# Last mixture: rows fetched by indirect DMA through a slot table, two dense tiles in front, weights split in the attention

## The reference

```
logits = x2 @ router_w;  probs = softmax(logits);  top_p, top_e = top_k(probs, 2)
for every chosen (token, expert e):
    h = gelu(x2[token] @ w_in[e] + b_in[e])
    y = (h @ w_out[e] + b_out[e]) * p          # p: the probability of that choice
    out[token] += y
x = x + out
```

## Time and profile before

| | |
|---|---|
| timed runs | 896.3, 900.05, 902.11 us |
| profiled execution | span 906.0 us; no time of its own is given beside the span |
| TensorE | 836.0 us busy, 92% of the span, mean granted clock 0.958 |
| VectorE (DVE) | 670.9 us, 74% |
| ScalarE (ACT) | 485.3 us, 54% |
| GpSimd (POOL) | 251.8 us, 28% |
| DMA | 115.93 MB, mean 128 GB/s |

### The profile page before, as it was taken

How to read it: one execution, slowest core, us unless ns; L and a number is a source line. 1 busy time by engine, 2 the same in 40 slices (tenths; PEclk the granted TensorE clock), 3 DMA queues, 4 the chain that set the end, 5 groups by cost and what they waited for, 6 DMA issues and landing times. The chain is left out here.

```text
span 906.0 us, 17871 instructions
## 1 busy us (share of the span) xinstructions
PE 836.0 (92%) x6115; PEld 773.1 (85%) x6115; DVE 670.9 (74%) x1359; ACT 485.3 (54%) x1022; POOL 251.8 (28%) x211
## 2 busy tenths in 40 slices
PE   7988999998797999999999999979799878999977
PEld 5877899998587999999999999965788745989867
DVE  3883799998676447888888888968687777775657
ACT  2653333333373557677777777753455542645643
POOL 7420233223003550034433333330122201432530
PEclk8988999999898999999999999998899987999999
DMA  8990000000402228577777777725000040534325
GB/s 303 294 291 3 1 1 0 1 1 1 150 2 100 100 84 299 225 231 232 232 232 232 226 222 228 255 25 185 1 1 1 1 175 31 162 100 130 106 86 171
DMA packets 60067, 115.93 MB, mean 128 GB/s; under 512 B 8482, under 2 KB 45956, under 8 KB 53220
## 3 DMA queue, kind: packets, MB, share of 16 engines
q1 hardware_dynamic: 48420, 97.48, 32.4%
q0 software_dynamic: 9408, 15.53, 7.0%
q10 hardware_dynamic: 2176, 2.10, 0.7%
HBM read 84.29 MB, written 30.79 MB: 127 GB/s over the span
## 5 line engine op out<-in xcount | busy, mean ns | idle before, releaser
L143 PE MATMUL e_ps_h<-e_xh,e_w1h 128*128 128x256 f32 (+1 forms) x496 | 141.7, 286 | 5.5 <-issue 5.5
L144 PE MATMUL e_ps_h<-e_xl,e_w1h 128*128 128x256 f32 (+1 forms) x496 | 139.2, 281 | 0.0
L145 PE MATMUL e_ps_h<-e_xh,e_w1l 128*128 128x256 f32 (+1 forms) x496 | 138.9, 280 | 0.0
L1996 POOL DMA_INDIRECT accumulated<-m_yo,m_token x39 | 77.7, 1992 | 194.1 <-ACT m_yo L2136 166.4
L143 PE MATMUL e_ps_o<-e_w2h,e_hh 128*128 128x256 f32 x440 | 122.3, 278 | 0.0
L2116 ACT ACTIVATE e_hf<-e_ps_h,e_b1s 128x256 f32<-128x256 f32 (+1 forms) x248 | 97.9, 446 | 45.1 <-PE e_ps_h L145 42.2
L145 PE MATMUL e_ps_o<-e_w2h,e_hl 128*128 128x256 f32 x440 | 121.8, 277 | 0.0
L144 PE MATMUL e_ps_o<-e_w2l,e_hh 128*128 128x256 f32 x440 | 121.8, 277 | 0.0
L894 POOL TENSOR_TENSOR at_pr<-at_pr,at_inv 128x1168 f32<-128x1168 f32 (+2 forms) x48 | 58.7, 1238 | 225.9 <-DVE at_inv L826 225.9
L143 PEld LDWEIGHTS e_ps_h<-e_xh,e_w1h 128*128 128x128 f32 x496 | 94.9, 191 | 5.7 <-issue 5.7
L144 PEld LDWEIGHTS e_ps_h<-e_xl,e_w1h 128*128 128x128 f32 x496 | 94.9, 191 | 0.0
(11 more groups left out here) (427 smaller groups left out, 2338.3 us busy)
## 6 DMA issues: line engine op xcount, KB each, us to landing
e_w1s<-in_m_w SPq DMA_DIRECT2D x24, 1024.0 KB
e_w2s<-in_m_w SPq DMA_DIRECT2D x24, 1024.0 KB, 7.2
slots_in<-zero SPq DMA_DIRECT2D x20, 258.0 KB, 9.4
e_xin<-slots_in SPq DMA_DIRECT2D x16, 258.0 KB
last_slots_in<-zero SPq DMA_DIRECT2D x14, 258.0 KB, 7.7
d_xin<-last_slots_in SPq DMA_DIRECT2D x10, 258.0 KB
d_results<-last_results SPq DMA_DIRECT2D x10, 256.0 KB, 4.5
as_wk<-in_a_wk SPq DMA_DIRECT2D x2, 1024.0 KB, 9.2
```

Source lines behind the costliest of these rows:

```text
L143: nc.tensor.matmul(out, lh, rh, start=start, stop=False)
L144: nc.tensor.matmul(out, lh, rl, start=False, stop=False)
L145: return nc.tensor.matmul(out, ll, rh, start=False, stop=stop)
L1996: nc.gpsimd.indirect_dma_start(out=g.acc[a], out_offset=bass.IndirectOffsetOnAxis(ap=token[:, n, a:a + 1], axis=0), in_=yo[:, q, a, :], in ...
```

## The change

- **Dense tiles.** 2 tiles in front instead of 4 (`FRONT = 2`), 2 at the back as before. So 12 tiles are routed instead of 10: 12 pairs and 7 singles.
- **Weights.** A new class `Matrices` loads and splits all 16 weight matrices of the last mixture during the second attention: in each of 16 tiles ACT casts one matrix (128x512) after the exponential, and POOL subtracts after the normalisation. The loads and splits in `prepare` and in the dense front go.
- **Slot table.** Nothing is scattered before the routed tiles and no slots are zeroed. SP stores the normalised rows of tiles 0 to 11 to HBM in order (3 DMAs of 512 KB), with one row of zeros ahead. DVE makes one-hot tables of each choice's unit and lane; POOL multiplies the unit table with the row number; 24 matmuls (`find`) accumulate the row number of every slot. DVE turns that into two integer tables, `source` and `target`.
- **Fetch.** POOL fetches each block of 128 rows with an indirect DMA through `source`, 4 tiles ahead (`AHEAD = 4`), and stores results through `target`, in one program.
- **Front.** One semaphore step per expert; the low part of the hidden values is made on POOL; ACT scales the second product into its own buffer for each expert, and DVE adds the eight buffers to X during the routed tiles. The counts' product comes in turn 3 instead of turn 0, and `find` in turn 8, ahead of the last second product.
- **Results.** ACT no longer scales the routed results; DVE multiplies by the probability as it adds them at the end, in 6 parts of two tiles, four operations a part. The bias product for the dense tiles moves from the front to turn 3 of the back.

```diff
-        rows = self.g.xs1.rearrange("(a p) d -> p a d", p=P)
-        for a in range(0, rows.shape[1], 2):
-            sp.dma_start(rows[:, a:a + 2, :], self.g.zero[:]).then_inc(self.g.s_zeroed1, 16)
...
+            if matrices and (not static or 0 <= t < NT):
+                matrices.scalar(act, t, q)
...
+            if matrices:
+                matrices.gpsimd(pool, t, q)
...
+class Matrices:
+
+    COUNT = 2 * E
+
+    def __init__(self, nc, ctx, L, w, sem):
+        self.nc, self.w = nc, w
+        self.W = DK * L.hid
+        sb = lambda name, shape, dt=FP: ctx.enter_context(nc.sbuf_tensor("d_" + name, shape, dt))
+        self.high, self.low = sb("w_high", [P, self.COUNT, self.W], FR), sb("w_low", [P, self.COUNT, self.W], FR)
+        self.raw = sb("w_raw", [P, 2, self.W])
+        self.s_raw = [sem(f"d_w_loaded{q}") for q in range(2)]
+        self.s_high, self.s_low = sem("d_w_high"), sem("d_w_low")
+
+    def sync(self, sp):
+        for i in range(self.COUNT):
+            wait(sp, self.s_low, i - 1)
+            sp.dma_start(self.raw[:, i % 2, :], self.w["w2" if i % 2 else "w1"][i // 2]).then_inc(self.s_raw[i % 2], 16)
+
+    def scalar(self, act, i, q):
+        wait(act, self.s_raw[q], 8 * i + (8 if q else 16))
+        self.nc.scalar.copy(one(self.high, i), self.raw[:, q:q + 1, :]).then_inc(self.s_high, 1)
+
+    def gpsimd(self, pool, i, q):
+        wait(pool, self.s_high, i + 1)
+        self.nc.gpsimd.tensor_tensor(one(self.low, i), self.raw[:, q:q + 1, :], one(self.high, i), ALU.subtract).then_inc(self.s_low, 1)
+
+
     CT = 4
+    FRONT = 2
     REST = 2
-    DT = CT + REST
+    DT = FRONT + REST
     RT = NT - DT
...
+    SECOND = RT * P
+    EMPTY = TOPK * SECOND
+    UC = 32
+    AHEAD = 4
...
+                    sp.dma_start(g.xs1[0:1, :], g.zero[0:1, 0, 0:D]).then_inc(self.s_rows, 16)
+                    rows = g.xs1[1:1 + self.RT * P].rearrange("(t p) d -> p t d", p=P)
+                    for c in range(self.RT // CT):
+                        ts = slice(c * CT, (c + 1) * CT)
+                        sp.wait_ge(s_xn, CT * (c + 1))
+                        sp.dma_start(rows[:, ts, :], xn[:, ts, 0:D]).then_inc(self.s_rows, 16)
...
-        for i, is_it in enumerate((self.is1, self.is2)):
-            link(dve, v.tensor_tensor(tmp, slot, rows(is_it), ALU.mult))
-            link(dve, v.tensor_reduce(self.inv[:, 0:RT], tmp, AX.X, ALU.add))
-            v.tensor_copy(self.at[:, i, :], self.inv[:, 0:RT, 0]).then_inc(self.s_k, 1)
+
+        both = slot.rearrange("p (a t) e -> p a (t e)", a=1).to_broadcast([P, TOPK, RT * E])
+        link(dve, v.tensor_tensor(self.masked[:].rearrange("p c t e -> p c (t e)"), both,
+                                  self.chosen[:, :, 0:RT, :].rearrange("p c t e -> p c (t e)"), ALU.mult))
+        link(dve, v.tensor_reduce(self.at[:], self.masked[:].rearrange("p c t e -> p (c t) e"), AX.X, ALU.add))
+        link(dve, v.tensor_copy(self.at_i[:], self.at[:]))
+        link(dve, v.tensor_scalar(self.lane[:], self.at_i[:], P - 1, None, ALU.bitwise_and))
+        link(dve, v.tensor_tensor(self.unit[:], self.at[:], self.lane[:], ALU.subtract))
+        v.tensor_tensor(self.is_unit[:], self.unit[:].to_broadcast([P, TOPK * RT, self.UC]),
+                        self.unit_no[:].to_broadcast([P, TOPK * RT, self.UC]), ALU.is_equal).then_inc(self.s_is, 1)
+        for i in range(TOPK):
+            ns = slice(i * RT, (i + 1) * RT)
+            v.tensor_tensor(self.lanes[:, ns, :], self.lane[:, ns, :].to_broadcast([P, RT, P]),
+                            self.lane_no[:].to_broadcast([P, RT, P]), ALU.is_equal).then_inc(self.s_lanes, 1)
...
+        dve.wait_ge(self.s_found, 1)
+        v.tensor_copy(self.row[:], ps_i)
+        link(dve, v.tensor_scalar(self.back[:], ps_i, self.SECOND + 0.5, -float(self.SECOND), ALU.is_gt, ALU.mult))
+        link(dve, v.tensor_tensor(self.back[:], self.row[:], self.back[:], ALU.add))
+        v.tensor_copy(self.source[:], self.back[:]).then_inc(self.s_source, 1)
+        link(dve, v.scalar_tensor_tensor(out=self.none[:], in0=self.row[:], scalar=0.5, in1=self.empty_no[:], op0=ALU.is_lt, op1=ALU.mult))
+        link(dve, v.scalar_tensor_tensor(out=self.none[:], in0=self.row[:], scalar=-1.0, in1=self.none[:], op0=ALU.add, op1=ALU.add))
+        v.tensor_copy(self.target[:], self.none[:]).then_inc(self.s_target, 1)
...
+                    def find(i):
+                        if i == 0:
+                            pe.wait_ge(s_units, 1)
+                        pe.wait_ge(self.s_lanes, i + 1)
+                        for n in range(i * RT, (i + 1) * RT):
+                            last = nc.tensor.matmul(ps_i, self.lanes[:, n, :], unit_rows[:, n, :], start=n == 0, stop=n == TOPK * RT - 1)
+                        if i == TOPK - 1:
+                            last.then_inc(self.s_found, 1)
...
+                        if r == 1:
+                            pe.wait_ge(r_b1, TILES)
+                            nc.tensor.transpose(ps_w, wt[:, RT:NT, :].rearrange("p t e -> p (t e)"), g.ident[:]).then_inc(s_wtt, 1)
+                        if r == 3:
+                            pe.wait_ge(s_wtt_sb, 1)
+                            pe.wait_ge(self.s_b, 16 * 3)
+                            for a in range(0, DT, 2):
+                                last = nc.tensor.matmul(ps_b[:, a // 2], wtt[:], b2d[0:DT * E, a:a + 2, :], start=True, stop=True)
+                            last.then_inc(s_bias, 1)
...
+                    def weighted(r):
+                        if r == 0:
+                            act.wait_ge(s_wt, 1)
+                        act.wait_ge(s_m2, r + 1)
+                        for a in range(FRONT):
+                            last = a_.activation(fy[:, r, a, :], ps_o[:, r % 4, a, :], ACT.Copy, scale=wt[:, FULL + a, r:r + 1])
+                        last.then_inc(s_ev, 1)
...
                     def add_results(i):
                         each = RT // PARTS
-                        ts = slice(i * each, (i + 1) * each)
-                        x = g.X[:, ts, :]
                         dve.wait_ge(s_y[i], 32)
-                        v.tensor_tensor(x, x, y[:, 0, ts, :], ALU.add).then_inc(s_sum, 1)
-                        dve.wait_ge(s_sum, i + 1)
-                        v.tensor_tensor(x, x, y[:, 1, ts, :], ALU.add).then_inc(s_fin, 1)
+                        for c, (p, added) in enumerate(((self.p1, s_sum), (self.p2, s_fin))):
+                            if c:
+                                dve.wait_ge(s_sum, i + 1)
+                            for t in range(i * each, (i + 1) * each):
+                                x = g.X[:, t, :]
+                                last = v.scalar_tensor_tensor(out=x, in0=y[:, c, t, :], scalar=p[:, t], in1=x, op0=ALU.mult, op1=ALU.add)
+                            last.then_inc(added, 1)
+                        if r == E - PARTS:
+                            dve.wait_ge(s_bias, 1)
+                            dve.wait_ge(s_x, E)
+                            x = g.X[:, FULL:NT, :]
+                            v.tensor_tensor(x, x, ps_b[:, 1], ALU.add).then_inc(s_bias_x, 1)
+                        if r == E - PARTS + 1:
+                            dve.wait_ge(b_x, REST * r)
+                            x = g.X[:, RT:FULL, :]
+                            v.tensor_tensor(x, x, ps_b[:, 0], ALU.add).then_inc(s_bias_x, 1)
+                            dve.wait_ge(s_bias_x, 2)
...
+                    gp = nc.gpsimd
+
+                    def low_hidden(r):
+                        pool.wait_ge(s_hh, r + 1)
+                        wait(pool, s_m2, r - 1)
+                        gp.tensor_tensor(hl[:, r % 2], hf[:, r % 2], hh[:, r % 2], ALU.subtract).then_inc(s_hl, 1)
+
+                    def fetch(n):
+                        for a in range(rows_of(n)):
+                            u = first_dma(n) + a
+                            gp.indirect_dma_start(
+                                out=xin[:, n % AHEAD, a, :], out_offset=None, in_=g.xs1,
+                                in_offset=bass.IndirectOffsetOnAxis(ap=self.source[:, u:u + 1], axis=0)).then_inc(s_in[n % AHEAD], 16)
+
+                    for r in range(E):
+                        low_hidden(r)
+                    pool.wait_ge(self.s_is, 1)
+                    gp.tensor_tensor(unit_rows[:], self.is_unit[:], self.row_no[:].rearrange("p c (t a) -> p (c t) a", a=1).to_broadcast([P, TOPK * RT, UC]),
+                                     ALU.mult).then_inc(s_units, 1)
+                    pool.wait_ge(self.s_source, 1)
+                    for n in range(AHEAD):
+                        fetch(n)
+                    pool.wait_ge(self.s_target, 1)
                     k = 0
                     for n in range(TILES):
-                        pool.wait_ge(r_ys, n + 1)
+                        if n + AHEAD < TILES:
+                            pool.wait_ge(r_tr, n + 1)
+                            fetch(n + AHEAD)
```

(57 more changed lines are left out.)

277 lines of the change are left out of this document (95 added, 182 removed).

## The result

Timed: 929.48 us (925.2 to 932.42, four runs) against 900.74 of the kernel before: ratio 1.032, 95% interval 1.028 to 1.035. The change makes the kernel 28.7 us slower; forecast were +14.1 us (914) in a range of 897 to 930. The profiled execution took 925.2 us; its span is 923.1, so 2.1 us lie around the span.

The account below looks back on a forecast made before the run. The routed part was taken to be bound by a two-tile loop through POOL's in-order queue. 879.6 + 35.7 + 4.8 = 920.1 against a 906.0 span, +14.1 on 900.05, gives 914 us; range 897 to 930.

Parts of the forecast that it names:

- The loop of two tiles through POOL's queue: Routed part: a later fetch stands behind a store that needs an earlier result; 12.0 us for two tiles.
- rival A: Routed part: the two-tile loop does not close, only POOL's rate counts; 889 us timed, chance 0.13.
- Rival B: Loop closes, but landing 1.6 us, no low clock, DVE hides the tail's waits; 901 to 906 us, chance 0.22.
- rival C: Routed part: TensorE at 1.2 GHz at nearly every tile's start, some 20 us instead of 4.8; 929 timed, chance 0.12.
- First fetch: Dense front: first fetch at 781.3, bounds 779 and 785, with the mixture started at 750.0.
- Routed part: Routed tiles: last result 98.3 us after the first fetch, at 879.6 against 876.9 before.
- The clock term: Routed part: three of six long pauses drop TensorE's clock, 1.6 us each; 4.8 us, ends 0 and 10.
- Tail: Dense back and results: DVE rounds of 3.45 us; 35.7 us after the last result instead of 29.1.
- the split: Second attention: 16 casts on ACT and 16 subtractions on POOL fit into free room; no cost.
- Rival D: Second attention: the weight split lands on its chain; +10 us, so 924, chance 0.05.
- The zeroing DMAs: First setup: removing 14 zeroing DMAs, for which nobody waits before the last mixture; zero.

Follow-up runs that it names:

- ahead5: The changed kernel with five tiles fetched ahead instead of four; 905.55 us, 1.004 of the kernel before.
- ahead8: The changed kernel with eight tiles fetched ahead instead of four; 900.85 us, 1.000 of the kernel before.
- nolow: The changed kernel with POOL's hidden low-part subtraction cut to 8 of 256 columns in six of the front's eight experts; 927.66 us, 1.028 of the kernel before.
- front8: ahead8 with the counts' product in turn 2, the unit table multiplied on DVE and the find behind the last second product; 899.40 us.
- ring: front8 with four result buffers instead of two in the routed part; 893.27 us, 0.990 of the kernel before.
- warm9: The changed kernel with nine matmuls that only keep TensorE busy before the fetch waits of tiles 5, 7, ... 15; 923.59 us, 1.026.
- double: The changed kernel with ACT casting each weight matrix twice in the second attention; 935.06 us, 1.038 of the kernel before.
- spare: The changed kernel with 14 zeroing DMAs put back at the end of the first setup, into an unread buffer; 931.25 us, 1.032.
- before2: The kernel before, unchanged, run again with a second profile of its own; 899.55 us.

## Why the prediction was right in kind and wrong in size

**The mechanism was right.** The loop of two tiles through POOL's queue closes, and undoing it (ahead5, ahead8) gives the whole loss back. So rival A, in which the loop does not close, is out. Rival B is out too: its conditions were a landing of 1.6 us (here 1.96 in the double turn) and no low clock (here 5.5 us). That 929.48 is the 929 of rival C, just inside the stated range, is luck: C laid 20 us on the low clock, which cost 5.5, and the other terms made up the rest.

In the profiled executions the last mixture takes 179.6 us against 156.0: +23.6, where +14.1 were forecast. The 9.5 us between them are, by the prediction's steps:

- **First fetch: 37.8 us after the start, forecast 31.3: +6.5. This step failed.** It read "From there DVE needs as now to 765.38, 9.4 us", and it costed POOL's eight subtractions and its multiplication as POOL time alone. But the subtractions hold up small DVE operations of that chain: from the counts to the unit table 16.4 us, forecast 11.8, of which nolow gives back 4.3. The counts were 1.1 us late as well. So the unit table, not the last hidden low part (26.8), releases the multiplication, 2.8 us after the 25.5 of the forecast. The multiplication takes 2.93 us, not 1.9 (+1.0), and here it is DVE that holds up POOL. The multiplication begins beside DVE's first operation on the lane tables (1.75 us, from 771.71 to 773.46) and ends at 774.81, 1.35 us after it. In nolow it begins beside the second one, which ends at 773.77, and ends at 775.11, 1.34 us after that. In the changed kernel the second lane operation in turn takes 3.03 us instead of 1.75 and ends 1.6 us after the multiplication. In both executions the two engines, first in the changed kernel, then in nolow:

```profile
771.71 4.70 DVE L1228 TENSOR_TENSOR d_lanes<-d_lane,d_lane_numbers 128x1536 fp32r<-128x1536 int32 x2
771.88 2.93 POOL L1648 TENSOR_TENSOR d_unit_rows<-d_is_unit,d_row_numbers 128x768 fp32r<-128x768 f32 x1 [1.53 <-DVE d_is_unit L1224]
```

```profile
770.33 3.44 DVE L1228 TENSOR_TENSOR d_lanes<-d_lane,d_lane_numbers 128x1536 fp32r<-128x1536 int32 x2
772.12 2.99 POOL L1649 TENSOR_TENSOR d_unit_rows<-d_is_unit,d_row_numbers 128x768 fp32r<-128x768 f32 x1
```

What the multiplication takes with DVE idle, no run shows. The find takes 5.3 us for 24 matmuls, not 2.5 (+2.8), as TensorE had waited 5.86 us and ran at 1.2 GHz; the clock had been charged to the routed part only. Placed behind the last second product and at the high clock, the find took 3.1 us in front8. In ring, in the same order, it took 5.1 at 1.2 GHz, so the placing alone does not hold the clock.

- **Routed part: 110.0, forecast 98.3 and 4.8 of clock: +6.9.** The clock term was near: 5.5 by warm9. Rival C was right that TensorE falls to 1.2 GHz after nearly every long wait (the first rows after the five waits of 4.2 to 5.2 us are slow), and wrong in its price. Of the 13.46 us of the double turn shown above, TensorE has 5.50 instead of 3.95 (the clock), DVE and hand-over 0.97 (0.96), four DMAs 5.03 (4.8), the landing 1.96 (2.2). With the clock at 1.00 the three double turns still take 0.7 us more than forecast each, the singles and the end 2.5 us more together, and the first tiles 1.5, at a clock of 0.75. Why warm9's turns alternate between 13.2 and 11.8 us stays open.
- **Tail: 31.8, forecast 35.7: -3.9.** The round is 3.09 us, not 3.45, as four additions in a row take 1.79 us; and the first additions came 2 us sooner, because the low clock of the earlier trace rows did not recur.

The Trainium skill ("TensorE: Matmul & The Clock Gate", HAM oscillation) states that tiles whose work is shorter than the wait for the next load start cold every time. The trace agrees that tiles start cold: the four transposes take 1.01 to 1.11 us after the waits of 4.2 us and more, 0.60 without a wait. It shows this although TensorE works longer than it waits (busy 28.2 of the 42 us from 806 to 848). It puts the price at some 1.5 us for two tiles.

**The rest of the 28.7 us.** The execution of the kernel before that was read took 908 us (its span and the 2.1 around one), 7 above the median, and its mixture takes 153.4 us in the other profile. So the mixture costs 23.6 to 26.2 us more. The stage from the second attention to the front takes 110.6 and 110.9 us in the two profiles before, 111.0 to 112.6 in the executions with the split: about 1.2 us, which had been costed at nothing. Together these are 25 to 27.4 us, at the lower end of the interval of the ratio (25 to 32 us); what makes up the rest stays open.

Rival D was rightly put low: most of the first cast fitted into the room, and double shows that a second one does not. The zeroing DMAs bring nothing, as costed (spare). The row stores and the scaling taken off ACT were not tried apart.

## What to carry to other kernels

Where one in-order queue both fetches inputs and stores results, follow a fetch back through that queue: if it stands behind a store that needs the previous fetch, the depth of prefetch is less than it looks, and one more buffer may be worth more than any faster part. Cost an operation moved to POOL also at what DVE runs beside it, in both directions. And check which stretch a pause puts at the low clock, short chains of small matmuls above all.

## What the runs showed of the hardware

**POOL's arithmetic and DVE's hold each other up.** Five DVE operations of 0.17 to 0.26 us that met a POOL subtraction ended within 0.11 us of its end, and POOL's multiplication ended 1.35 us after the DVE operation that it met. It was not every DVE operation: the reduction at 759.73 and the copy of one element per partition at 760.05 run beside POOL's at their usual 0.29 and 0.15 us, the 128x7 addition behind them waits. The Trainium skill ("SBUF — State Buffer", "SBUF: two separate sides") says why: VectorE and GpSimd share a pair of ports as an exclusive lock, which whoever starts first holds for a whole instruction while the other is blocked. VectorE takes it for an operation in a two-port mode, or for one with two SBUF inputs beside a GpSimd operation that reads SBUF. Trace and nolow agree. The same is seen in the first setup. In the first profile of the kernel before, and then in the changed kernel:

```profile
5.08 4.38 DVE L437 TENSOR_SCALAR as_al<-as_al 32x4 f32<-32x4 f32 x1
```

```profile
5.11 0.54 DVE L434 TENSOR_SCALAR as_al<-as_al 32x4 f32<-32x4 f32 x1
```

A POOL memset of 3.7 us begins at 5.57 in both, and the long one ends 0.2 us after it. It was long again in before2 (4.28 us) and in front8's profile (4.24), and in none of the other profiles. The short one ends at 5.65, just as the memset before that one does (5.64). In the three profiles with the long one the first attention starts at 83.1 to 85.3 us, in the others at 79.2 to 81.3. It does not settle where the last mixture starts, though: in before2 that is at 743.25 us. Why the operation waits for the second memset in some executions is not shown.

**Indirect DMAs.** In the changed kernel a gather of 128 rows of 1 KB holds POOL 0.95 to 0.99 us (the first one 1.04), and a store 0.96 to 0.99, or 1.18 to 1.19 in four of the five cases where POOL had waited for the data of a tile of two blocks. Between two of them lie 0.30 us where POOL waits for nothing. Where TensorE waited for fetched rows, it went on 1.7 to 2.0 us after the end of the second gather of a tile, once 2.8, and 2.2 to 2.3 us after a single one.
